# A macaron block on one core: the maxima's rows on ScalarE's DMA queue, query loads with two semaphores, and a planner with longer transfer times

## The reference

```python
x = x + 0.5 * ffn(layernorm(x))            # ffn: fft, sparse complex weight, ifft, real part, + bias
x = x + attention(layernorm(x))            # 16 heads of 8, causal, one key/value head for all
x = x + 0.5 * ffn(layernorm(x))
```

```python
latent = x @ Wc_down
q = (latent @ Wq_up).reshape(B, T, 16, 8)
k, v = split(latent @ Wkv_up)              # 8 columns each
att = softmax(causal(q k^T / sqrt(8)))     # over the keys
y = (att v).reshape(B, T, 128) @ Wc_proj
```

## Time and profile before

| | us |
|---|---|
| median of 3 runs | 639.36 (635.91 to 642.02) |
| the profiled execution, own time | 643.32 |
| its span, first to last instruction | 641.2 |
| TensorE busy | 604.1, granted clock 0.949 in the mean |
| VectorE busy | 501.0 |
| ScalarE busy | 382.5 |
| GpSimd busy | 89.7 |

### The profile page before, as it was taken

One profiled execution on the slowest core, in us unless ns is written; L12 is line 12 of the kernel. 1 busy time (PEld: TensorE's weight loads), 2 busy tenths in 40 slices (PEclk: granted clock), 3 DMA queues, 4 the chain that ended last, 5 costly groups with the idle time before them and its releaser, 6 DMA issues.

```text
span 641.2 us, 13530 instructions
## 1 busy us (share of the span) xinstructions
PE 604.1 (94%) x5249; PEld 336.3 (52%) x5249; DVE 501.0 (78%) x1306; ACT 382.5 (60%) x834; POOL 89.7 (14%) x311
## 2 busy tenths in 40 slices
PE   7687999999999999989999699999999999999897
PEld 6563755645454556544455365545454645453347
DVE  4662999998999989884999569999988989887113
ACT  2324146576777676744776367676766776676651
POOL 4111111200011304200011212300002020001100
PEclk8777999999999999995999879999999999999789
DMA  5011210011010110011010100001010100000000
GB/s 173 7 39 65 81 37 1 4 62 41 1 39 2 40 42 3 19 62 40 2 40 1 40 26 17 3 29 68 25 38 4 55 1 19 3 2 2 18 1 17
DMA packets 16978, 18.68 MB, mean 29 GB/s; under 512 B 2427, under 2 KB 14555, under 8 KB 16915
## 3 DMA queue, kind: packets, MB, share of 16 engines
q1 hardware_dynamic: 16243, 17.47, 8.1%
q10 hardware_dynamic: 672, 0.36, 0.2%
HBM read 11.90 MB, written 5.24 MB: 27 GB/s over the span
## 4 chain that ended last, share of the span: by engine, by line
PE 78%; ACT 7%; DVE 7%; DMA 4%; issue 2%; SPq 1%; POOL 0%; ACTq 0%; DVEq 0%
PE o_ps L764 21%; PE s1p L714 19%; PE st L738 18%; ACT probs L858 5%; PE st L742 4%; PE misc L644 4%; PE s1p L717 4%; PE st L750 3%; DMA q_sb<-mT 3%; DVE mx_pair L1015 2%; DVE mx L1015 1%; ACT z L840 1%; PE misc L639 1%; DMA wkv<-in_w_kv 1%; PE misc L674 1%
## 5 line engine op out<-in xcount | busy, mean ns | idle before, releaser
L858 ACT ACTIVATE probs<-st 128x512 f32<-128x512 f32 (+2 forms) x640 | 308.7, 564 | 164.1 <-PE st L742 105.8
L1015 DVE TENSOR_REDUCE mx_pair<-s1p 128x1 f32<-128x512 f32 (+3 forms) x432 | 261.5, 663 | 47.7 <-PE s1p L714 34.3
L738 PE MATMUL st<-q_sb,k_sb 75*128 75x512 bf16 (+3 forms) x768 | 221.7, 336 | 14.6 <-DMA q_sb<-mT 9.4
L714 PE MATMUL s1p<-k_sb,q_sb 72*128 72x512 bf16 (+3 forms) x768 | 223.2, 337 | 6.0 <-issue 3.4
L764 PE MATMUL o_ps<-probs,v_sb 128*32 128x512 f32 (+3 forms) x1536 | 151.5, 514 | 0.0
L738 PEld LDWEIGHTS st<-q_sb,k_sb 75*128 75x128 bf16 x768 | 75.8, 100 | 89.3 <-ACT probs L858 35.0
L714 PEld LDWEIGHTS s1p<-k_sb,q_sb 72*128 72x128 bf16 x768 | 74.8, 101 | 90.9 <-DVE mx_pair L1015 34.2
L1015 DVE TENSOR_REDUCE mx<-s1p 128x2 f32<-128x256 f32 (+2 forms) x192 | 104.3, 594 | 13.2 <-PE s1p L717 11.8
L742 PE MATMUL st<-causal,ident 128*128 128x128 bf16 x512 | 103.6, 226 | 0.0
L717 PE MATMUL s1p<-ident,causal 128*128 128x128 bf16 x512 | 101.2, 224 | 0.0
L764 PEld LDWEIGHTS o_ps<-probs,v_sb 128*32 128x32 f32 x1536 | 41.1, 112 | 71.1 <-issue 63.0
(11 more groups left out here) (115 smaller groups left out, 362.5 us busy)
## 6 DMA issues: line engine op xcount, KB each, us to landing
q_sb<-q_parts_dram SPq DMA_DIRECT2D x31, 288.0 KB
q_parts_dram<-q_parts SPq DMA_DIRECT2D x24, 128.0 KB
x_sb<-in_x SPq DMA_DIRECT2D x8, 256.0 KB, 4.8
out<-out_sb SPq DMA_DIRECT2D x8, 256.0 KB, 2.3
q_sb<-mT SPq DMA_DIRECT2D x14, 24.0 KB
const<-in_consts SPq DMA_DIRECT2D x1, 320.0 KB, 5.0
q_sb<-q_parts SPq DMA_DIRECT2D x5, 32.0 KB
q_sb<-q_parts ACTq DMA_DIRECT2D x4, 32.0 KB
```

Source lines behind the costliest of these rows:

```text
L714: last = mm(ps[:, e * width:(e + 1) * width], queries[:, h0 + e, at:at + P], k_sb[0:ROWS, b, lo:lo + width], start=True, stop=not diagonal)
L738: last = mm(ps[:, e * w:(e + 1) * w], k_sb[0:ROWS_MAX, b, P * ki:P * ki + P], q_sb[0:ROWS_MAX, slot, c, h0 + e, first:BLK], start=True, st ...
L858: nc.scalar.activation(probs[:, s % PROBS, h0:h0 + per, 0:w], st[n % 3][:, 0:per * w].rearrange("p (e w) -> p e w", e=per), ACT.Exp, scale ...
L1015: v.tensor_reduce(dst, s1p[n % 3][:, 0:heads * width].rearrange("p (e w) -> p e w", e=heads), axis=AX.X, op=ALU.max).then_inc(s1_free, 1)
```

## The change

Three edits. (1) The function `max_rows` moves from SP's program into ScalarE's: wait for `mT_ready`, then one DMA. The plan's item for it is now called `rows` and stands where the SP item stood, right after the post step of the mT job; ScalarE takes it in its turn. (2) `q_loaded` becomes two semaphores per slot, one for each half; TensorE waits for half 0 ahead of a unit's first sweep-1 tile and for half 1 ahead of tile N1_HALF. (3) The planner counts a loaded half 0 as due 6.5 us and half 1 as due 10.5 us after the load item (both 6.0 before), and puts the load item 6.0 us after the store item (3.0 before).

```diff
-LOAD_STEP, STORE_STEP, MAX_STEP = 6.0, 3.0, 2.5
+LOAD_STEP, STORE_STEP, MAX_STEP = (6.5, 10.5), 6.0, 2.5
...
-            self.q_at[0][1] = self.pe + LOAD_STEP
+            self.q_at[0][1] = self.pe + LOAD_STEP[0]
...
-        self.q_at[u] = [self.pe + LOAD_STEP] * 2
+        self.q_at[u] = [self.pe + t for t in LOAD_STEP]
...
-            self.items.append(("sp", "max", u, part))
+            self.items.append(("rows", u, part))
...
-        q_loaded = [sem(f"q_loaded{n}") for n in range(SLOTS)]
+        q_loaded = [[sem(f"q_loaded{n}_{c}") for c in range(2)] for n in range(SLOTS)]
...
-                             .broadcast_to([PARTS, PARTS * HD, GH * BLK])).then_inc(q_loaded[u % SLOTS], 16)
+                             .broadcast_to([PARTS, PARTS * HD, GH * BLK])).then_inc(q_loaded[u % SLOTS][c], 16)
...
-            def max_rows(u, part, turn):
-
-                sp.wait_ge(mT_ready, seen(mT_ready))
...
-                elif item[1] == "max":
-                    max_rows(item[2], item[3], turn % 2)
-                    turn += 1
...
-                        pe.wait_ge(q_loaded[slot], 32 * (u // SLOTS) + (32 if slot else 16))
+                        pe.wait_ge(q_loaded[slot][0], 16 * (u // SLOTS) + (16 if slot else 0))
...
-                    if u == 0:
-                        pe.wait_ge(q_loaded[0], 16)
+                    pe.wait_ge(q_loaded[slot][1], 16 * (u // SLOTS + 1))
...
+            def max_rows(u, part, turn):
+
+                act.wait_ge(mT_ready, seen(mT_ready))
+                slot = u % SLOTS
+                if part == 2:
+                    nc.scalar.dma_start(q_sb[ROWS:ROWS_MAX, slot, :, :, :].rearrange("a c h t -> a (c h t)"), mT[turn][:, :]
+                                 ).then_inc(max_loaded[slot], 16)
+                else:
+                    nc.scalar.dma_start(q_sb[ROWS:ROWS_MAX, slot, part, :, :].rearrange("a h t -> a (h t)"),
+                                 mT[turn][0:PARTS * GH * NT // 2, :]).then_inc(max_loaded[slot], 16)
...
+                elif item[0] == "rows":
+                    max_rows(item[1], item[2], turn % 2)
+                    turn += 1
```

More of the change, by code:

```diff
@@ L593, in _ @@
             store_q(0)
-            first, turn = True, 0
             for item in plan:
@@ L842, in normalise @@
                 ins.then_inc(z_ready[n], 1)
+            def max_rows(u, part, turn):
[7 more added lines that the diff above has]
+                                 mT[turn][0:PARTS * GH * NT // 2, :]).then_inc(max_loaded[slot], 16)
+            turn = 0
             nc.scalar.dma_start(bias_in[:, :], bias.unsqueeze(0).broadcast_to([P, D])).then_inc(bias_loaded, 16)
@@ L1006, in post @@
                     dot(mT_ready)
-            max_order = [item[2:] for item in plan if item[0] == "sp" and item[1] == "max"]
+            max_order = [item[1:] for item in plan if item[0] == "rows"]
             def sweep1_max(n, u, t):
```

## The result

| | us |
|---|---|
| median after (4 runs) | 666.9 (666.0 to 668.8) |
| median before (4 runs) | 640.2 (635.9 to 642.0) |
| ratio, 95% interval | 1.0431, 1.0373 to 1.0489 |

The account below looks back on a forecast made before the run. The prediction took TensorE, busy 94% of the span, as the bound, its time lost in two waits for maxima and the low clock behind them. It summed -15.5 + 7 + 0 - 1.5 = -10 to a median of 629.5 us, range 619 to 645.

Parts of the forecast that it names:

- What bounds the kernel: TensorE, busy 94% of the span; time is won only where it stands still or runs slowly.
- step 1: Two waits of TensorE for maxima behind query loads, with half clock after: cost 15.4 to 21.7 us, taken as 17.
- The count from below: Intervals between maxima on SP's queue against intervals of other units: 8.2 and 7.2 us lost, sum 15.4.
- Step 2: Maxima on ScalarE's queue get in between the load's two halves: gain 15.5 us, ends 0 and 17.
- Rival B: At two handovers the queues share without passing, maxima still land about 8 us after issue: +5.5, 645 us; chance 0.2.
- Step 3: 18 waits and issues in ScalarE's program delay its work: 7 us lost on TensorE, ends 0 and 15.6.
- Step 4: Split load semaphore: TensorE waits for a load only at the first; 15 more wait instructions, taken as 0 us.
- Step 5: Planner's new times move the first second-half sweep of u=0 and some loads: gain 1.5 us, ends -1 and 3.
- rival D: Another plan order puts the loads of u=8 and u=11 after the maxima, giving A's gain; A or D 0.25.
- The sum: Whole change: -15.5 + 7 + 0 - 1.5 = -10 us, median 629.5 us.

Follow-up runs that it names:

- e4_swap: The kernel before, with SP issuing the loads of units 8 and 11 behind the maxima instead of ahead of them; 619.9 us, ratio 0.9672.
- e7_wide: The kernel before, with each half of a query load as three DMAs of 24 rows in place of one; 615.0 us, ratio 0.9587.
- e1_queue: The kernel before with only the maxima's rows moved to ScalarE's queue, planner and semaphores as before; 661.8 us, ratio 1.0336.
- e13_act_hold: e9_wide_act, with SP waiting at the old place of the maxima's issue until they have landed; 634.3 us, ratio 0.9897 to the kernel before.
- e9_wide_act: e7_wide with the maxima's rows issued on ScalarE's queue, planner as before; 639.8 us, ratio 0.9965 to the kernel before.
- e6_actwait: e4_swap, with SP still issuing the maxima but ScalarE also waiting for mT_ready; 627.9 us, ratio 0.9805 to the kernel before.
- e2_times: The kernel before with only the planner's longer load and store times; 654.5 us, ratio 1.0212.

## Why the prediction was wrong, step by step

- **What bounds the kernel: right, and step 1 undersized.** The meetings and the low clock were the thing to gain; e4_swap is worth 21.2 us by itself. The sum took 17 of 15.4 to 21.7. The count from below had intervals of other units as its measure, 29.9 us and 106.4 for three; without the meetings the same intervals are 9.4 and 9.9 us shorter, not 8.2 and 7.2. The list of losses lacked one: the half clock behind the wait for the first load, 5.5 us with it (e7_wide).
- **Step 2, another queue: failed.** "I take the middle: it gets in between the two halves" gave 15.5 us; measured 0: no wait went (12.9 us in e1_queue, 9.4 before). The maxima land just behind the second half of the load, 7.7 to 10.4 us after issue. Rival B had the mechanism: "the load keeps its engines and the maxima still land about 8 us after issue". What misled were the first transfers: they pass each other, but over 16 engines and with packets of about 0.5 KB on both sides. Here small packets alternate on three engines with packets 16 times as large, and they begin only when the first half is through. The rule that the prediction quoted from the Trainium skill ("DMA: Bandwidth & Descriptors", "Issuing engines are not separate DMA queues") is what this trace shows: both queues run on the same engines and interleave. The other rule it quoted, that engines alternate between rings by whole packets, stands in the Trainium skill (same page, "Queues, rings and completion order") with about 9 to 17 descriptors to a packet as typical. The trace shows a finer turn: 4 to 6 rows of 4 KB and as many of 256 B in every 0.3 us on three engines, where nine rows of 4 KB on one engine would take 1.4 us. Here the measurement decides.
- **Step 3, ScalarE: right in place, wrong in size.** 7 us were taken, between 0 and 15.6; measured about 15 (e13_act_hold and e9_wide_act by their intervals), the upper end. Two of the delays can be read off and are as worked out: the normalisations stand 3.1 us for `dve_dot` once, with the old order at unit 5 (in the changed kernel's order it is at unit 9), and the exponential at unit 12 is 1.8 us late. What was missing is the clock: stops of about 2 us are enough for a short stretch at 1.2 GHz. The prediction's sum let the clock fall only behind stops as long as those of before. The wait alone makes 8.0 (e6_actwait, with the old loads); that the issue of 0.75 us behind it, which lengthens each delay, makes the rest is inferred, as no kernel had the issue without the wait.
- **Step 4, the semaphores: right.** 0.9987.
- **Step 5, the planner: failed.** "Gain 1.5; ends -1 and 3"; measured a loss of 13.4. The expected gain at the start hardly came: in e2_times the maxima of unit 0's second half go out at 87.2 in place of 87.4. (They go at 85.6 in the changed kernel and at 85.1 in e1_queue, so that is the queue's doing.) And a plan moved by 3.5 us put the ends of other units next to other loads, and three maxima meet a load in place of two. The prediction named such shifts and priced them at the ends of the range as ties, not as a whole meeting with its half clock, 10 us each by its own step 1. Its rival D had loads that move off the maxima; they moved onto them.
- **The sum.** Step 2: 0; step 3: 15; step 5: 13.4; together 28.4, against 26.7 measured. With loads of three DMAs 15 and 4.0 stand against 20.7 for the whole. The sign turned with step 2 alone; rival B's 645 was still 22 short for steps 3 and 5.

## What to carry to other kernels

A second DMA queue gives a small urgent transfer no right of way over a large one on the same DMA engines; it even takes away the one it has by standing first in a shared queue. Look instead at what the large one does: spread it over more engines (e7_wide, 26 us) or issue it behind the small one on the same queue (e4_swap, 21 us). Both are changes of a few lines that add nothing to the program of a busy engine. And before a wait for a slower engine is put into the program of an engine that feeds TensorE, count what is queued behind it, and add the clock to each stop of TensorE.

## What the runs showed that I had not expected

- Two queues on the same three engines took turns packet by packet, 52 to 53, whatever their size. And the maxima had no packet at all for at least 3.7 us after their issue, until the first half of the load was through, where alone they land within 2.7 us. Why the start is held back (the making of the descriptors or the engines) was not settled.
- Two transfers issued in the same moment on two queues: the small one took 10.3 us; 0.9 us apart on one queue, small one first: in use 4.3 us after the issue, no wait.
- Behind a stop of TensorE of 2.04 us (e13_act_hold, unit 12) the granted clock was 0.50 for 3.4 us; behind the stops of 5.1 to 6.0 us of the changed kernel it stayed there for 11 to 14 us.
- The intervals between maxima repeat between kernels with the same plan to 0.02 us (from unit 1's to unit 2's 28.73, 28.74 and 28.73 us in e7_wide, e9_wide_act and e13_act_hold). A loss can so be laid on its interval by a subtraction. This also shows what an experiment brings in by itself, as the 4.0 us of e13_act_hold at the first load, which a comparison of medians puts on ScalarE.
